# A new order at the entry of the second retrieval feed-forward's loop: copies taken earlier, four filler products, one table load ahead of a wait

## The chip, the cores and the metric

The kernel runs on one core of one Trainium2 chip. The metric is device microseconds of that core. Before the change three runs gave 1164.84, 1164.48 and 1162.4 us, median 1164.48 us. One further execution was profiled; the rows below are from it.

## The reference, cut to what matters

The program is four pairs of layers on x (16 sequences of 256 rows, 128 wide, f32): cross attention, then a feed-forward, each added to x after a layer norm. The change touches the entry of the third feed-forward, which the kernel calls `f2`:

```python
def _L2_ffn_ref(hidden_states, Wg, bg, Wu, bu, Wd, bd, Wq, keys, down_embed, up_embed):
    q = (hidden_states @ Wq).reshape(b, t, 2, H, RET // 2)
    sim = jnp.einsum('btphn,hkpn->pbthk', q, keys)
    sc, ix = jax.lax.top_k(sim, KPH)            # 8 best of 64, two sides, 4 heads
    ...
    all_sc = (sx[..., :, None] + sy[..., None, :]).reshape(b, t, H, KPH * KPH)
    scores, pk = jax.lax.top_k(all_sc, KPH)     # 8 best of the 64 pairs
    ...
    w = jnp.einsum('btd,bthkd->bthk', hidden_states, de)
    w = jax.nn.silu(w) * jax.nn.softmax(scores, axis=-1)
    experts_states = jnp.einsum('bthk,bthkd->btd', w, ue)
    mlp = jax.nn.silu(hidden_states @ Wg + bg) * (hidden_states @ Wu + bu) @ Wd + bd
    return mlp + experts_states
x = x + _L2_ffn_ref(_layernorm(x, axis=-1), ...)
```

Everything is f32 at this place. The work of later layers (attention `a3`, feed-forward `f3`) follows.

## The kernel before, in words

The 4096 rows are 32 tiles of 128 rows, and 8 groups of 4 tiles. The stages stand one behind the other in the program of each engine: `a2` (the attention ahead of `f2`), `f2`, `a3`, `f3`. Each engine runs its own program in the order in which it is written, and semaphores tie the engines together. There is no scheduler: the order in the code is the order on the engine.

In `f2` the work on a group g is spread over two turns of the loop. The *scores* of group g are made a turn ahead: TensorE multiplies the turned rows `hT` with `simw` (L1919, `sims` in `f2_pe`, four products, all through PSUM bank 0), ScalarE copies each from PSUM to SBUF (L2022, `sims` in `f2_act`), VectorE takes the eight best (L1838, L1850), GpSimd forms all sums of pairs (L2116, `pairs`), ScalarE takes exponentials (L2045, `exps`, four heads for each of four tiles), and VectorE weighs them (L2193, `weigh`). The *products* of group g (L1940, L1943, L1947 on TensorE, four columns c of three products) go to ScalarE for two Silu each (L2072, L2074) and to VectorE (L2228). GpSimd also folds the weighed exponentials (L2126, L2131) and adds the bias rows (L2137).

`groups2` runs the body in a loop for groups 0 to 5 (two to a pass) and then written out for groups 6 and 7. Ahead of it stands the entry, which is what the change touches:

- On TensorE: turning group 1's normalised rows (L336, `T(1, 1)`), then `sims(1, 1, t)` for t = 0 to 3. Each of these waits until ScalarE has emptied bank 0; the first waits for `hT`.
- On ScalarE: in `f2_first_act`, still in `a2`, three copies of `a3`'s values (L683). Then in `f2_act` `logs(0)` (L2027, L2031), `logz(0)` (L2035), and for each tile t the four exponentials of group 0 and behind them the copy `sims(1, t, 0)` (L2022). Behind the exponentials of tile 0 stand the end of a layer norm (L307, L310, L311), the fourth copy of `a3`'s values (L683) and `take_turned` (L341), which copies the turned rows from bank 0 to `hT`.
- On VectorE: `z`, `shift`, the rest of a layer norm (up to L293), `weigh(0, t)`; then the body, which begins with `top(1, 0)`.
- On GpSimd: 16 `pairs` of group 0, `bias(0)`, then folds and pairs in turn.

The functions Exp and Ln share one table of ScalarE, Silu is in another. Each body therefore loads a table twice: ahead of its first Silu (in the profile under L2072) and, through `preload_act_table_set`, behind its last (L2078).

Of the kernel before, what the change touches and what calls it, by code (L numbers as in the profile page):

```python
# [29 lines left out]
P = 128  # L30
# [3 lines left out]
GT = 4  # L34
# [44 lines left out]
def build(nc, dram):  # L79
    with ExitStack() as ctx:  # L80
        def sb(name, shape, dt=F32):
            return ctx.enter_context(nc.sbuf_tensor(name, shape, dt))
# [3 lines left out]
        def S(name):  # L86
            if name not in sems:
                sems[name] = ctx.enter_context(nc.semaphore(name))
            return sems[name]
# [24 lines left out]
        ident = W["ident"]  # L114
# [6 lines left out]
        simw = sb("simw", [P, 512])  # L121
# [25 lines left out]
        def bank(i):  # L147
            return psum[:, i, :]

        def tile_of(A, t):  # L150
            return A[:, ds(t, 1), :].rearrange("p a b -> p (a b)")
# [40 lines left out]
        def sem(s, name):  # L192
            return S("all_" + name)

        def at(s, name):
            return sum(count(x, name) for x in SUB[:SUB.index(s)])
# [142 lines left out]
        def take_turned(act, s, g, j):  # L339
            act.wait_ge(sem(s, "turned"), at(s, "turned") + g + 1 + 2)  # L340
            act.activation(hT[:, j, :], bank(0), ACT.Copy).then_inc(sem(s, "hT"), 1)  # L341
# [1567 lines left out]
        def f2_pe(pe, a3):  # L1909
            s = "f2"  # L1910
# [12 lines left out]
            for t in range(GT):  # L1923
                sims(1, 1, t)

            def dense_out(g, c):

                if c == 0:
                    pe.wait_ge(sem(s, "res"), at(s, "res") + g + 1)
                pe.wait_ge(S("f2_aT"), 4 * g + c + 1 + 1)  # L1930
                for t in range(GT):
                    pe.matmul(bank(7)[:, t * P:(t + 1) * P], aT[:, c, t * P:(t + 1) * P],
                              W["f2_wd"][:, c * P:(c + 1) * P], start=(t == 0 and c == 0), stop=False,
                              skip_group_check=True)
# [76 lines left out]
        def f2_act(act, a3):  # L2011
            s = "f2"
            act.sem_inc(S("f2_sl"), 1)
            act.sem_inc(S("f2_sg"), 1)

            def sims(G, t, before=None):
                act.wait_ge(S("f2_sim_ps"), 4 * G + t + 1)
                if before is not None:

                    act.wait_ge(S("f2_S"), 4 * before + t + 1)  # L2020
                    act.wait_ge(S("f2_t1"), 32 * before + 8 * t + 8)
                act.activation(sim[:, t * 512:(t + 1) * 512], bank(0), ACT.Copy).then_inc(S("f2_sim"), 1)  # L2022

            def logs(G):

                act.wait_ge(S("f2_m"), G + 1)
                act.activation(e8.rearrange("p t h k -> p (t h k)"), e8.rearrange("p t h k -> p (t h k)"), ACT.Exp)\  # L2027
                    .then_inc(S("f2_e8"), 1)
                if not (isinstance(G, int) and G == 0):
                    act.wait_ge(S("f2_mw"), 16 * G)  # L2030
                act.activation(best2, lead2, ACT.Copy).then_inc(S("f2_b2"), 1)  # L2031

            def logz(G):
                act.wait_ge(S("f2_z"), G + 1)
                act.activation(lnz2, z2, ACT.Ln).then_inc(S("f2_lnz"), 1)  # L2035

            def exps(G, t):

                if t == 0:
                    act.wait_ge(S("f2_shift"), G + 1)  # L2040
                act.wait_ge(S("f2_S"), 4 * G + t + 1)
                for h in range(NH2):
                    if not (isinstance(G, int) and G == 0 and 4 * t + h < 2):
                        act.wait_ge(S("f2_mw"), 16 * G + 4 * t + h - 1)
                    act.activation(bank(EX_BANK + h % 2), ssum[t][:, h * 512:(h + 1) * 512], ACT.Exp,  # L2045
                                   bias=shift2[:, t * NH2 + h:t * NH2 + h + 1]).then_inc(S("f2_ew"), 1)

            def norm(g, j):
                act.wait_ge(sem(s, "turned"), at(s, "turned") + g + 1)
                for t in range(GT):  # L2050
                    ins = act.activation(hrow[:, j, t * P:(t + 1) * P], tile_of(X, 4 * g + t), ACT.Identity,
                                         scale=rstd[:, ds(4 * g + t, 1)], bias=shifted[:, ds(4 * g + t, 1)])
                ins.then_inc(sem(s, "normed"), 1)

            logs(0)
            logz(0)
            for t in range(GT):
                exps(0, t)
                if t == 0:
                    ln_finish_act(act, s, 1)  # L2060
                    a3.values(3, 4)
                    take_turned(act, s, 1, 1)
                sims(1, t, 0)
            act.wait_ge(sem(s, "ln"), at(s, "ln") + 2 * LN_STEPS)

            def body(g, j, one_more, two_more):
                act.wait_ge(S("f2_pwT"), 4 * g + 1)
                for c in range(4):
                    act.wait_ge(S("f2_g_ps"), 4 * g + c + 1)
                    if c:  # L2070
                        act.wait_ge(S("f2_aT"), 4 * g + c)
                    act.activation(sl[c % 2], bank(3), ACT.Silu, bias=col("f2_bg%d" % c)).then_inc(S("f2_sl"), 1)  # L2072
                    act.wait_ge(S("f2_e_ps"), 4 * g + c + 1)
                    act.activation(sgT[:, c, :], bank(5), ACT.Silu).then_inc(S("f2_sg"), 1)  # L2074
                    if c == 1 and two_more:
                        norm(g + 2, j)
                if one_more:
                    act.preload_act_table_set("natural_log_exp_and_others")  # L2078
                if two_more:
                    take_turned(act, s, g + 2, j)  # L2080
                if one_more:
                    logs(g + 1)
                    logz(g + 1)
                if not one_more:
                    act.preload_act_table_set("natural_log_exp_and_others")
                    act.wait_ge(S("f2_S"), 4 * N_GROUPS)
                    act.wait_ge(S("f2_mw"), 16 * N_GROUPS)
                    a3.keys16(0)
                    take_turned(act, "a3", 0, 0)
                    a3.takeQ(0)  # L2090
                    a3.takeQ(1)
                    a3.keys16(1)
                    take_turned(act, "a3", 1, 1)
                    a3.takeN(0)
                for t in range(GT):
                    if one_more:
                        exps(g + 1, t)
                        if t == 0 and not two_more:
                            ln_finish_act(act, "a3", 0)
                    if two_more:  # L2100
                        sims(g + 2, t, g + 1)

            groups2(act, body)

        def f2_pool(pool):
# [869 lines left out]
```

## Time and profile before

| | |
|---|---|
| runs | 1162.4 to 1164.84 us, median 1164.48 |
| profiled execution | 1169.59 us, its span 1167.8 us |
| PE busy | 939.7 us, 80% |
| DVE busy | 836.0 us, 72% |
| ACT busy | 647.1 us, 55% |
| POOL busy | 464.6 us, 40% |

PE is TensorE, PEld its weight loads, DVE VectorE, ACT ScalarE, POOL GpSimd. Busy shares are averages over the whole span. `f2` lies between about 600 and 850 us of it, its entry between about 599 and 621 us. In a timeline, a row is: start in us, duration in us, engine, line, operation, output<-input with shapes, count; in square brackets the idle time before it and what ended that. Where instructions overlap in an engine's pipeline, a row's start can lie before the end of the row above.

### The profile page before, as it was taken

How to read it: one execution, taken by the hardware profiler on the slowest of the kernel's cores; microseconds unless marked ns; L12 is line 12 of the kernel's file. 1: busy time of each engine (PE TensorE's matmuls, PEld its weight loads, DVE VectorE, ACT ScalarE, POOL GpSimd, SP SyncE). 2: the span in 40 equal slices, each digit the busy share in tenths (PEclk: the TensorE clock that was granted, in tenths of full speed). 3: DMA queues.
4: the chain of work that ended last, by engine and by line, in shares of the span. 5: the costliest groups of instructions: out<-in, count | busy, mean ns of one | idle time of the engine just before them, and what ended most of it. 6: DMA issues, size and time to landing. Idle time of an engine off the chain costs nothing.

```text
span 1167.8 us, 21022 instructions
## 1 busy us (share of the span) xinstructions
PE 939.7 (80%) x7158; PEld 630.9 (54%) x7158; DVE 836.0 (72%) x2078; ACT 647.1 (55%) x1143; POOL 464.6 (40%) x446
## 2 busy tenths in 40 slices
PE   5958800578997998799859999998879988948987
PEld 3753300554555776355435767666645556527976
DVE  6785699857886666377778999999758885513443
ACT  4425578945653454566448778775456644104543
POOL 5500000001220001344369999998212242463655
PEclk9889955779999999799978999999979997978999
DMA  8000000055000000000000000000000000124431
GB/s 288 1 1 1 1 0 0 1 169 176 1 2 1 1 1 1 1 1 2 2 1 2 1 0 0 0 0 1 1 1 2 2 2 1 49 90 118 113 90 34
DMA packets 24233, 33.76 MB, mean 29 GB/s; under 512 B 3484, under 2 KB 20389, under 8 KB 23888
## 3 DMA queue, kind: packets, MB, share of 16 engines
q1 hardware_dynamic: 20720, 26.20, 7.3%
q0 software_dynamic: 3424, 6.38, 1.6%
q8 instruction: 55, 0.90, 0.3%
q14 instruction: 34, 0.28, 0.1%
HBM read 18.34 MB, written 15.98 MB: 29 GB/s over the span
## 4 chain that ended last, share of the span: by engine, by line
PE 35%; DVE 29%; issue 8%; ACT 5%; another core or an unknown queue 1%; POOL 1%; DVEq 1%; DMA 0%; POOLq 0%; ACTq 0%; SPq 0%
DVE big L850 7%; DVE hq L845 7%; PE psum L619 5%; PE psum L2534 5%; PE psum L1602 3%; ACT psum L2045 2%; DVE big L2193 2%; PE psum L2550 2%; PE psum L573 2%; PE psum L1619 2%; DVE big L854 2%; DVE psum L1850 1%; DVE tmp L1838 1%; DVE psum L1838 1%; PE psum L2436 1%
## 5 line engine op out<-in xcount | busy, mean ns | idle before, releaser
L845 DVE TENSOR_REDUCE hq<-psum 128x16 f32<-128x1024 f32 x96 | 114.5, 1220 | 82.1 <-PE psum L573 44.3
L2116 POOL TENSOR_TENSOR big<-big 128x512 f32<-128x512 f32 x128 | 128.7, 1050 | 7.0 <-ACT big L1878 7.0
L2193 DVE SCALAR_TENSOR_TENSOR big<-big,tmp,psum 128x512 f32<-128x512 f32 x128 | 90.4, 743 | 7.8 <-ACT psum L2045 4.7
L2045 ACT ACTIVATE psum<-big,tmp 128x512 f32<-128x512 f32 x128 | 84.9, 686 | 19.6 <-DVE big L2193 16.9
L735 ACT ACTIVATE big<-psum 128x1024 f32<-128x1024 f32 x64 | 62.0, 1021 | 54.6 <-PE psum L603 54.6
L850 DVE RECIPROCAL big<-psum 128x256 f32<-128x256 f32 x48 | 84.0, 1749 | 5.1 <-PE psum L619 4.9
L483 POOL TENSOR_TENSOR big<-big,w_const 128x256 f32<-128x256 f32 x32 | 24.0, 750 | 152.9 <-PE psum L619 145.8
L2721 DVE SCALAR_TENSOR_TENSOR big<-psum,big 128x128 f32<-128x128 f32 x118 | 36.0, 347 | 64.4 <-issue 45.3
L2126 POOL TENSOR_TENSOR big<-big 128x1024 f32<-128x1024 f32 x32 | 75.4, 2366 | 15.8 <-DVE big L2193 15.8
L1516 PE MATMUL psum<-f_downT,tmp 128*128 128x128 f32 x192 | 24.9, 294 | 68.0 <-DVE tmp L1399 68.0
L2414 POOL DMA_INDIRECT out<-big x59 | 57.9, 982 | 54.0 <-issue 34.2
L619 PE MATMUL psum<-big 128*32 128x256 f32 x768 | 52.3, 389 | 25.8 <-DVE big L854 25.7
L1285 DVE TENSOR_REDUCE amax<-big 128x1 f32<-128x1536 f32 x32 | 55.8, 1748 | 21.4 <-ACT big L1425 21.4
L599 PE MATMUL psum<-hq,big 32*128 32x256 f32 x768 | 65.6, 428 | 6.2 <-DVE hq L845 6.0
L341 ACT ACTIVATE hT<-psum 128x512 f32<-128x512 f32 x56 | 33.3, 595 | 58.0 <-PE psum L336 58.0
L2534 PE MATMUL psum<-tmp,big 128*128 x236 | 63.1, 391 | 0.9 <-ACT big L2581 0.8
L1516 PEld LDWEIGHTS psum<-f_downT,tmp 128*128 128x128 f32 x192 | 24.5, 210 | 68.8 <-DVE tmp L1399 68.3
L491 POOL TENSOR_TENSOR big<-big,w_a 128x256 f32<-128x256 f32 x16 | 11.7, 728 | 120.0 <-ACT big L707 120.0
L1258 POOL PARTITION_ALL_REDUCE qs<-qs x4 | 1.5, 371 | 144.7 <-DVEq L1238 131.1
L336 PE MATMUL psum<-w_const,hrow 128*128 128x128 f32 x224 | 37.4, 293 | 22.1 <-DVE hrow L1309 11.8
L483 POOL TENSOR_TENSOR big<-w_f,w_const 128x256 f32<-128x256 f32 x16 | 12.6, 791 | 105.5 <-PE psum L619 82.6
L1972 PEld LDWEIGHTS psum<-w_const,big 128*128 128x128 f32 x384 | 47.3, 196 | 8.6 <-issue 8.6
(334 smaller groups left out, 2629.2 us busy)
## 6 DMA issues: line engine op xcount, KB each, us to landing
rows<-pad SPq DMA_DIRECT2D x1, 7670.0 KB, 33.0
big<-rows SPq DMA_DIRECT2D x59, 130.0 KB
tmp<-in_pack_f SPq DMA_DIRECT2D x1, 2050.5 KB, 9.2
w_f<-in_pack_f SPq DMA_DIRECT2D x1, 1280.0 KB, 12.6
tmp<-in_pack_once SPq DMA_DIRECT2D x1, 960.0 KB, 7.1
out<-big POOLq DMA_INDIRECT x59
X<-in_x SPq DMA_DIRECT2D x1, 768.0 KB, 5.3
w_a<-in_pack_a SPq DMA_DIRECT2D x3, 256.0 KB, 8.1
```

The lines of the kernel that those rows point to most:

```text
L599: pe.matmul(bank(1 + r)[:, 256 * e:256 * e + 256], L.kbd[rows, b, e * P:(e + 1) * P], L.qT[b % L.ahead][rows, :], start=True, stop=False)
L619: ins = pe.matmul(bank(6)[32 * r:32 * r + 32, 256 * which:256 * which + 256], w, L.pt[b % 2][:, (2 * r + e) * 256:(2 * r + e + 1) * 256], ...
L735: act.activation(L.pt[b % 2][:, 1024 * half:1024 * half + 1024], psum[:, 1 + 2 * half:3 + 2 * half, :].rearrange("p c n -> p (c n)"), ACT.Exp,
L845: dve.tensor_reduce(nm, psum[:, 1 + 2 * t:3 + 2 * t, :].rearrange("p c (r l k) -> p (c r) l k", r=2, k=SK), AX.X, ALU.max, negate=True).th ...
L850: dve.reciprocal(L.rz, bank(6)[:, 256:512]).then_inc(hs("rz"), 1)
L1285: dve.tensor_reduce(amax[:, i, g:g + 1], A[:, g, :], AX.X, ALU.max, apply_absolute_value=True).then_inc(S("f0_am"), 1)
L2045: act.activation(bank(EX_BANK + h % 2), ssum[t][:, h * 512:(h + 1) * 512], ACT.Exp, bias=shift2[:, t * NH2 + h:t * NH2 + h + 1]).then_inc( ...
L2116: ins = pool.tensor_tensor(ssum[t][:, h * 512:(h + 1) * 512].rearrange("p (i j) -> p i j", i=ROWS2), st[:, 0, h, 0:ROWS2].unsqueeze(2).to_ ...
L2126: pool.tensor_tensor(ew[t][:, 0:left], ew[t][:, 0:left], ew[t][:, NFOLD * 512:], ALU.add)\
L2193: dve.scalar_tensor_tensor(out=ew[t][:, blk], in0=ssum[t][:, blk], scalar=best2[:, t, h, 7:8], in1=bank(EX_BANK + h % 2), op0=ALU.is_ge, o ...
L2414: pool.indirect_dma_start(dram["out"], bass.IndirectOffsetOnAxis(slot3[j % RS][:, ID3:ID3 + 1].bitcast(U32), 0), out3[j % RS], None, bound ...
L2534: ins = pe.matmul(bank(2 + j % 2)[:, 2 * P * k:2 * P * (k + 1)], hTb[j % 3], W["f3_w"][:, ds(weights_at(j, k), 2 * P)], start=True, stop=True)
```

## The change

It does three things. On ScalarE the fourth copy of values and `take_turned` move from behind the exponentials of tile 0 to the head of `f2_act`, the first copy `sims(1, 0, 0)` goes between `logs(0)` and `logz(0)`, and in the loop over tiles the copy of the next tile, not of the same, follows the exponentials. On TensorE four products of 256 columns into bank 6 follow the entry's `sims`; their result is not used. And each body of ScalarE begins with a load of the Silu table.

```diff
@@ f2_pe @@
             for t in range(GT):
                 sims(1, 1, t)
 
+            for _ in range(4):
+                pe.matmul(bank(6)[:, 0:2 * P], ident, simw[:, 0:2 * P], start=True, stop=True)
+
@@ f2_act @@
+            a3.values(3, 4)
+            take_turned(act, s, 1, 1)
             logs(0)
+            sims(1, 0, 0)
             logz(0)
             for t in range(GT):
                 exps(0, t)
                 if t == 0:
                     ln_finish_act(act, s, 1)
-                    a3.values(3, 4)
-                    take_turned(act, s, 1, 1)
-                sims(1, t, 0)
+                if t + 1 < GT:
+                    sims(1, t + 1, 0)
             act.wait_ge(sem(s, "ln"), at(s, "ln") + 2 * LN_STEPS)
 
             def body(g, j, one_more, two_more):
+                act.preload_act_table_set("silu_and_others")
                 act.wait_ge(S("f2_pwT"), 4 * g + 1)
```

On ScalarE, at the entry, this stood in a row before, up to the first copy of a score and not further (the three copies of values, L683, stand ahead of it, and after it exponentials and copies alternate; the last is a copy):

```order
L2027 ACTIVATE tmp<-tmp 128x128 [waits f2_m]
L2031 ACTIVATE tmp<-psum 128x128
L2035 ACTIVATE tmp<-tmp 128x16 [waits f2_z]
L2045 ACTIVATE psum<-big,tmp 128x512 [waits f2_S,f2_shift]
L2045 ACTIVATE psum<-big,tmp 128x512
L2045 ACTIVATE psum<-big,tmp 128x512 [waits f2_mw] x2
L307 ACTIVATE lnw<-lnw 128x8 [waits all_var]
L310 ACTIVATE psum<-lnw 128x8 [waits all_lnv]
L311 ACTIVATE lnw<-lnw 128x8
L683 ACTIVATE w_f<-psum 128x512 [waits att_v_ps]
L341 ACTIVATE hT<-psum 128x512 [waits all_turned]
L2022 ACTIVATE big<-psum 128x512 [waits f2_t1,f2_S,f2_sim_ps]
```

Line numbers of the changed kernel are up to 6 higher (L2025 is the copy, L2048 the exponential). There, at the same place, stands:

```order
L683 ACTIVATE w_f<-psum 128x512 [waits att_v_ps] x4
L341 ACTIVATE hT<-psum 128x512 [waits all_turned]
L2030 ACTIVATE tmp<-tmp 128x128 [waits f2_m]
L2034 ACTIVATE tmp<-psum 128x128
L2025 ACTIVATE big<-psum 128x512 [waits f2_t1,f2_S,f2_sim_ps]
L2038 ACTIVATE tmp<-tmp 128x16 [waits f2_z]
L2048 ACTIVATE psum<-big,tmp 128x512 [waits f2_S,f2_shift]
L2048 ACTIVATE psum<-big,tmp 128x512
L2048 ACTIVATE psum<-big,tmp 128x512 [waits f2_mw] x2
L307 ACTIVATE lnw<-lnw 128x8 [waits all_var]
L310 ACTIVATE psum<-lnw 128x8 [waits all_lnv]
L311 ACTIVATE lnw<-lnw 128x8
```

Three instructions (L683, L341 and the first copy) have moved ahead of the first exponential. Behind the exponentials of tile 0 only the layer norm's three stay, and behind those of tile 3 nothing stays.

Still on ScalarE, at the head of the loop's body, before:

```order
L163 UNCONDITIONAL_BRANCH [waits all_ln]
L163 ISA
L2072 ACT_TABLE_LOAD [waits f2_g_ps]
L2072 ACTIVATE big<-psum,w_const 128x512 [waits f2_pwT]
L2074 ACTIVATE big<-psum 128x512 [waits f2_e_ps]
```

And in the changed kernel (L2072 is now the line of the load itself, L2078 the Silu):

```order
L163 UNCONDITIONAL_BRANCH [waits all_ln]
L2072 ACT_TABLE_LOAD
L2073 ISA
L2078 ACTIVATE big<-psum,w_const 128x512 [waits f2_g_ps,f2_pwT]
L2080 ACTIVATE big<-psum 128x512 [waits f2_e_ps]
```

The load no longer waits for TensorE's first product (`f2_g_ps`); the number of loads is the same.

On TensorE, between the entry's score products and the loop:

```order
 L1919 MATMUL psum<-simw,hT 128x512 [waits f2_sim,all_hT] x4
+L1927 MATMUL psum<-simw,w_const 128x256 x4
 L163 UNCONDITIONAL_BRANCH [waits all_ln]
 L163 ISA
-L1940 MATMUL psum<-hT,w_f 128x512 [waits f2_sl]
+L1943 MATMUL psum<-hT,w_f 128x512 [waits f2_sl]
```

Nothing else of TensorE's order moves; the four fillers wait for nothing but their place in the queue. The orders of VectorE and GpSimd are as before.

## Rows read from the trace of the kernel before

**Rows 1.** The chain that ended last, in `f2`'s entry: start, us, what.
```profile
606.79 2.09 PE psum L1919 x2
...
619.80 0.85 ACT L2072
```

**Rows 2.** Timeline of ACT, the entry and the first body's load.
```profile
599.49 0.31 ACT L2027 ACTIVATE tmp<-tmp 128x128 f32<-128x128 f32 x1 [4.19 <-DVE tmp L1854]
...
601.67 0.22 ACT L2035 ACTIVATE tmp<-tmp 128x16 f32<-128x16 f32 x1 [1.71 <-DVE tmp L2177]
...
605.67 0.58 ACT L683 ACTIVATE w_f<-psum 128x512 f32<-128x512 f32 x1
606.15 0.59 ACT L341 ACTIVATE hT<-psum 128x512 f32<-128x512 f32 x1
608.90 0.60 ACT L2022 ACTIVATE big<-psum 128x512 f32<-128x512 f32 x1 [2.16 <-PE psum L1919]
609.39 1.29 ACT L2045 ACTIVATE psum<-big,tmp 128x512 f32<-128x512 f32 x2
...
618.83 0.58 ACT L2022 ACTIVATE big<-psum 128x512 f32<-128x512 f32 x1
619.80 1.28 ACT L2072 ACT_TABLE_LOAD   x1 [0.39 <-PE psum L1940]
```

**Rows 3.** Timeline of PE, the entry and group 0's first products.
```profile
597.69 0.60 PE L336 MATMUL psum<-w_const,hrow 128*128 128x128 f32 x4
606.79 2.08 PE L1919 MATMUL psum<-simw,hT 128*128 128x512 f32 x2 [8.49 <-ACT hT L341]
...
616.28 2.04 PE L1919 MATMUL psum<-simw,hT 128*128 128x512 f32 x2 [1.24 <-ACT big L2022]
618.11 1.60 PE L1940 MATMUL psum<-hT,w_f 128*128 128x512 f32 x2
...
621.83 1.13 PE L1940 MATMUL psum<-hT,w_f 128*128 128x512 f32 x2 [0.41 <-ACT big L2072]
622.80 1.02 PE L1943 MATMUL psum<-hT,w_f 128*128 128x512 f32 x2
```

**Rows 4.** Timeline of DVE, the entry and group 0's first product.
```profile
606.68 0.17 DVE L293 SCALAR_TENSOR_TENSOR lnw<-psum,lnw 128x8 f32<-128x8 f32 x1
610.19 0.75 DVE L2193 SCALAR_TENSOR_TENSOR big<-big,tmp,psum 128x512 f32<-128x512 f32 x1 [3.34 <-ACT psum L2045]
...
619.84 0.60 DVE L1838 MAX8 tmp<-big 128x8 f32<-128x64 f32 x4 [0.16 <-DVE big L2193]
...
621.91 0.75 DVE L2228 SCALAR_TENSOR_TENSOR big<-psum,w_const,big 128x512 f32<-128x512 f32 x1 [0.49 <-ACT big L2072]
```

**Rows 5.** Stretches: length, busy PE PEld DVE ACT POOL, granted clock, DMA share, GB/s.
```profile
598.00:600.00 2.00, 0.29 (x3) 0.05 (x1) 1.97 (x11) 0.47 (x2) 2.00 (x3) 0.70 0.00 0
618.00:620.00 2.00, 2.00 (x5) 0.89 (x4) 1.75 (x8) 1.61 (x4) 2.00 (x3) 0.68 0.02 4
858.00:860.00 2.00, 1.92 (x20) 1.52 (x24) 0.00 (x0) 0.70 (x2) 0.00 (x0) 0.50 0.04 8
```

**Rows 6.** Timeline of ACT, the loads of groups 1 and 7.
```profile
647.94 1.28 ACT L2072 ACT_TABLE_LOAD   x1
...
824.24 1.28 ACT L2072 ACT_TABLE_LOAD   x1 [1.75 <-PE psum L1940]
...
828.50 0.69 ACT L2072 ACTIVATE big<-psum,w_const 128x512 f32<-128x512 f32 x1 [1.79 <-PE psum L1940]
```

**Rows 7.** Timeline of POOL: folds of groups 0 and 1, bias of group 6.
```profile
613.21 2.36 POOL L2126 TENSOR_TENSOR big<-big 128x1024 f32<-128x1024 f32 x1 [4.70 <-DVE big L2193]
...
641.37 2.37 POOL L2126 TENSOR_TENSOR big<-big 128x1024 f32<-128x1024 f32 x1 [0.40 <-DVE big L2193]
...
807.66 1.27 POOL L2137 TENSOR_TENSOR X<-X,addrow 128x512 f32<-128x512 f32 x1
```

**Rows 8.** Timeline of DVE, behind the loop.
```profile
804.39 4.59 DVE L224 TENSOR_TENSOR lnw<-stats 128x20 f32<-128x20 f32 x1
```

## The prediction

> **What bounds the kernel now.** I read the chain of waits first. In the entry of `f2` it runs from ScalarE's copy of the turned rows into TensorE's first score product at 606.79 and ends, after copies, exponentials and products, in the table load at 619.80 [rows 1]. ScalarE's timeline shows why: ScalarE is idle 4.19 us ahead of `logs(0)` and 1.71 us ahead of `logz(0)`; then, behind the exponentials of tile 0, it copies values (605.67) and the turned rows (606.15), waits 2.16 us for the product that those rows feed, and copies that (608.90), before the exponentials of tile 1 start at 609.39 [rows 2]. So work that could have been done in an idle stretch stands between two exponentials. TensorE had the turned rows ready at 597.69 + 0.60 = 598.29 and then sat 8.49 us [rows 3]. VectorE waited 3.34 us for the exponential [rows 4], and GpSimd 4.70 us for VectorE [rows 7]. All four engines wait for this one detour. It happens once, not in each group.
>
> **The moved copies: what goes.** All times in this part are of the profiled execution.
>
> Values and turned rows. TensorE has long finished the values' product, and the turned rows are ready at 598.29. Both copies (0.58 and 0.59 us [rows 2]) fit into the 4.19 us in which ScalarE waits for VectorE: the turned rows' copy then runs from 598.35 to about 598.95, and `logs(0)` still starts at 599.49. Price: nothing, cover 0.5 us.
>
> The first score. TensorE starts it 0.05 us behind the copy, as it does now (606.15 + 0.59 = 606.74, start 606.79 [rows 2, 3]), so at 599.0. The granted clock falls within 598 to 600 (mean 0.70 [rows 5]), so I take the slower level, as today: from the product's start to the copy's start 608.90 - 606.79 = 2.11 us. The copy starts at 601.1, the next instruction 0.49 us behind (608.90 to 609.39), at 601.6. `logz(0)` waits for VectorE until 601.67 anyway [rows 2]. Hidden, but with 0.1 us of cover only; the bounds are 0 and +0.3 us (a product that starts a few tenths late). I take 0.
>
> Tile 0 to tile 1. The exponentials of tile 0 and the layer norm's three stay where they are, up to 605.67. Now the copy of tile 1's score comes, whose product has been done since 603.8 (it follows the first copy), and 0.49 us later, at 606.16, the exponentials of tile 1 start, instead of at 609.39: 3.23 us earlier. VectorE is free then: its layer norm ends at 606.68 + 0.17 = 606.85 [rows 4], and the exponential's first result comes at about 606.9, 0.8 us behind its start as today (609.39 to 610.19). Tiles 2 and 3 keep their pace, since their products of 2.1 us stand beside 3.3 us of exponentials.
>
> The end. The last copy (618.83, 0.58 us) is gone from behind tile 3, and so is the 0.39 us that the load waited for TensorE's first product [rows 2], if that product is there. ScalarE can load at 618.83 - 3.23 = 615.60 instead of 619.80: 4.20 us. The first Silu follows at 616.9 instead of 619.80 + 1.28 = 621.1.
>
> **Who is late next.** TensorE starts its fourth score product behind the copy ahead of tile 2's exponentials, at about 609.7 (now 616.28), done at 611.7. Then come the fillers. At the slower level the fourth score product took 618.11 - 616.28 = 1.83 us to the next one's start, 512 columns [rows 3]; four fillers of 256 columns are worth two such, 3.7 us, so at worst they end at 615.3. The loop's first product, another 1.8 us at that level, is then ready at 617.1, against a Silu at 616.9: 0.2 us at worst. But the clock should rise in the meantime. It rose from 1.2 to 2.4 GHz within 618 to 620 (mean 0.68 [rows 5]), while TensorE worked without a gap from 616.28 on. Here it works without a gap from 609.7 on, so I expect full clock while the fillers run, these done by about 614 and the three products of column 0 by about 616.6. The fillers stand in time in which TensorE would wait: they cost nothing, and gain little, as the clock would have risen on column 0's products too.
>
> VectorE has gained only 3.24 us: its `top(1, 0)` starts at 616.6 and takes until 618.2 (619.84 to 621.91 - 0.49 = 621.42 now [rows 4]), and group 0's first sum of products starts there instead of at 621.91: 3.7 us. TensorE's second column waits for the Silu and starts at 617.65 instead of 621.83 [rows 3]: 4.2 us. Nothing of TensorE waits for VectorE's first sum until four products later, and from 622 to 634 TensorE has no gap at all in the chain, so TensorE's 4.2 us count; VectorE makes up its 0.5 us out of 0.25 to 0.65 us waits that it has later in the group.
>
> GpSimd gains 3.3 us at its second fold (613.21) and runs without a gap from there to 641.37, where it waits 0.40 us for VectorE [rows 7]. It waits so at this fold in each group. So it is 0.9 us behind the others in group 0 and has made that up by group 2. No engine waits for it inside the loop: the list of waits from 620 to 820 us has no row with GpSimd as the releaser.
>
> **The table load ahead of the wait.** Load and Silu need each other only through ScalarE's own queue. In group 1 the load stands without idle time ahead of it (647.94 [rows 6]); it is so in groups 1 to 6, six loads. Putting it ahead of a wait that is already fulfilled gives nothing there. In group 0 the wait was the 0.39 us counted above. In group 7 the load waited 1.75 us for TensorE (824.24) and would now be done first, so the Silu comes 1.28 us earlier. But the Silu's own followers don't wait for it: TensorE has `a3`'s four key products behind column 0, and ScalarE's next Silu waits 1.79 us for TensorE [rows 6]. Value: 0, with bounds 0 and -1.3 us.
>
> The load takes 1.28 us in all rows, and the next instruction starts 0.01 us behind it. The Trainium skill, "ScalarE: Activation LUTs", section "What ACT_TABLE_LOAD costs", gives 1283 ns for the load and 1380 ns of drain, 2.66 us for each switch. The trace agrees on the load and shows no drain ahead of the 647.94 one. By that page hiding it in group 7 could be worth 2.66 us of ScalarE's time there.
>
> **Sum.** -3.23 (tile 1) - 0.58 (last copy) - 0.39 (wait) = -4.2 us for ScalarE and TensorE; +0.1 for the two places with hardly any cover. -4.1 us. Behind the loop VectorE is held 4.59 us at 804.39 [rows 8] until GpSimd's last instruction of the loop ends at 807.66 + 1.27 = 808.93 [rows 7]; as GpSimd has caught up by then, this shifts with the rest. What comes later depends on data alone and shifts too. On the profiled execution's own time 1169.59 becomes 1165.5; that execution lies 5.1 us over the median of the runs, so 1164.48 becomes 1160.4 us.
>
> **Rivals.**
>
> A. GpSimd decides. If its few tenths of slack are not there in the changed loop, its end at 808.93 moves only by the 3.3 us that it gains at its second fold, and VectorE behind it likewise: 1161.2 us. For it speaks that GpSimd works 641.37 - 0.40 - 613.21 = 27.8 us of a group of 647.94 - 619.80 = 28.1 us [rows 2, 6, 7]. Against it: the wait of 0.40 us, which comes again in each group. The Trainium skill, "SBUF — State Buffer", section "SBUF: two separate sides", gives the rule behind the held instruction: a VectorE operation with two inputs in SBUF and a GpSimd operation take one port pair, and the later one blocks. By that rule GpSimd's end sets VectorE's start at 808.93, which the rows bear out to 0.05 us.
>
> B. The gain is given back later. TensorE's clock changes level a dozen times between 800 and 1060 us, and each change can come a microsecond or so earlier or later against the shifted work. Half of the 4.1 us lost that way: 1162.5 us, no difference that can be told.
>
> C. The clock stays low. Column 0's last product then ends at 615.3 + 3 x 1.8 = 620.7, the second column starts 1.1 us earlier than now, and from there each 0.86 us product takes 1.72. If that holds through columns 1 to 3, nine products, it costs 7.7 us: -1.1 + 7.7 = +6.6, 1171 us, slower. It decides once the low level lasts beyond about 627.5 us (6.8 us, 3.4 us lost). For it: in 858 to 860 us TensorE was busy 1.92 of 2 us and still at 0.50 [rows 5], and a gap of 1 us waits at 616.6. Against it: that stretch had gaps around it, and in groups 1 to 6 gaps of 0.7 us left the clock at full.
>
> D. The load is worth more than I think: if ahead of the wait it hid in all eight groups, 7 x 1.28 = 9 us more, 1151 us. Against it: no idle time ahead of six of the loads.
>
> **How the numbers follow.** What a measurement of this kernel can tell is about 0.2%, 2.3 us, so faster means under 1162.2. Chances: my forecast (1159 to 1162) 0.70; A 0.09; B 0.13; C 0.04; D 0.03; nothing reaches the end at all 0.01. Forecast, A and D are faster, 0.82; B and the last mostly the same, 0.13 with a little left over; slower is C with a part of B's outcomes, 0.05. The range: the forecast with the bounds of the uncovered places (+0.3) and of group 7 (-1.3), a microsecond of scatter in the medians on either side, and up to B: 1157.8 to 1163.2.
>
> **What would show it.** In the changed profile: the turned rows' copy at about 598.4, the first score's copy at 601.1 ahead of `logz(0)`, tile 1's exponentials at 606.2, the load at 615.6 with no idle time ahead, the first Silu at 616.9; GpSimd's second fold at about 610; group 1's load at 643.7 (now 647.94); VectorE's held instruction at 800.2. I am wrong if `logz(0)` starts more than 0.3 us late, if the granted clock is at 0.50 beyond 617, or if the group from 643.7 on is longer than the 28.1 us of the group before it now.

## The result and the profile after

The changed kernel took 1158.60 us in the median of 8 runs (1154.26 to 1160.51), the kernel before 1163.45 us in 8 (1162.40 to 1164.87). The ratio is 0.9954, its 95% interval 0.9941 to 0.9966. So it is faster by 5.4 us (4.0 to 6.9), or 4.85 us from median to median; 4.1 us were forecast. The median of 1158.60 us lies within the range that was stated (1157.8 to 1163.2), but 0.4 us under the band of 1159 to 1162 us that was given the chance of 0.70; the kernel before came out 1.0 us under the median from which the forecast counted. Two later comparisons of the same kernel gave 0.9968 (0.9957 to 0.9980) and 0.9957 (0.9942 to 0.9972), 3.7 and 5.0 us.

The profiled execution took 1160.51 us, its span 1158.7 us. It is 9.1 us under the profiled execution of before, but that difference is not to be read as the change's: the kernel before, profiled again, took 1162.21 us (span 1160.4 us), 1.7 us more than the changed kernel's profile, which reached `f2` later. The first profile of before held stalls worth some 7 us behind 995 us that the second does not have (experiment 5). In the entry the two profiles agree to 0.01 us.

Executions differ ahead of `f2`: the changed kernel reaches its head 2.5 us later than before in this profile, the same kernel in experiment 12 0.2 us later, and over all fourteen profiles the start of `logs(0)` lies between 599.2 and 602.0 us. I therefore count from the start of `logs(0)` (599.49 before, 601.99 after). These are the rows of ScalarE after that answer to [rows 2] (start, us, operation, in brackets idle time before):

```profile
600.83 0.60 ACT L341 ACTIVATE hT<-psum 128x512 f32<-128x512 f32 x1 [2.16 <-PE psum L336]
601.99 0.31 ACT L2030 ACTIVATE tmp<-tmp 128x128 f32<-128x128 f32 x1 [0.56 <-DVE tmp L1854]
...
603.59 0.60 ACT L2025 ACTIVATE big<-psum 128x512 f32<-128x512 f32 x1 [1.12 <-PE psum L1919]
604.18 0.22 ACT L2038 ACTIVATE tmp<-tmp 128x16 f32<-128x16 f32 x1
...
608.18 0.58 ACT L2025 ACTIVATE big<-psum 128x512 f32<-128x512 f32 x1
608.66 1.29 ACT L2048 ACTIVATE psum<-big,tmp 128x512 f32<-128x512 f32 x2
...
618.18 1.28 ACT L2072 ACT_TABLE_LOAD   x1
619.48 0.69 ACT L2078 ACTIVATE big<-psum,w_const 128x512 f32<-128x512 f32 x1
...
646.52 1.28 ACT L2072 ACT_TABLE_LOAD   x1
```

The 2.16 us of waiting between two exponentials are gone. (The 2.16 us in the first row are another wait, for TensorE to turn the rows, in a stretch in which ScalarE would wait for VectorE anyway; that the two numbers are alike is chance.) And `logz(0)` (L2038) follows `logs(0)` by 2.19 us as against 2.18 us before. On TensorE, to set beside [rows 3]:

```profile
601.48 2.08 PE L1919 MATMUL psum<-simw,hT 128*128 128x512 f32 x2 [0.69 <-ACT hT L341]
...
612.26 2.04 PE L1919 MATMUL psum<-simw,hT 128*128 128x512 f32 x2 [1.31 <-ACT big L2025]
614.10 3.62 PE L1927 MATMUL psum<-simw,w_const 128*128 128x256 f32 x8
617.51 1.44 PE L1943 MATMUL psum<-hT,w_f 128*128 128x512 f32 x2
...
620.51 1.02 PE L1943 MATMUL psum<-hT,w_f 128*128 128x512 f32 x2
```

The fillers (L1927) and the loop's first products run without a gap, and the second column's product at 620.51 follows them with no wait: here TensorE, not the Silu at 619.48 + 0.69 = 620.17, decides. The chain of waits after says the same (start, us, what):

```profile
612.26 2.04 PE psum L1919 x2
614.31 3.41 PE psum L1927 x8
617.72 1.24 PE psum L1943 x2
```

The fillers stand on the chain, the list of waits that ended last. The clock, to set beside [rows 5] (length, busy time of PE, PEld, DVE, ACT, POOL, granted clock, DMA share, GB/s):

```profile
616.00:618.00 2.00, 2.00 (x6) 1.50 (x5) 1.90 (x5) 1.78 (x3) 2.00 (x3) 0.50 0.01 4
618.00:620.00 2.00, 2.00 (x5) 0.76 (x4) 1.84 (x11) 1.97 (x3) 2.00 (x2) 0.91 0.00 0
```

It rose only at about 618.4 (the mean of 0.91 over 618 to 620 puts it at 618.36), behind the fillers. GpSimd, to set beside [rows 7]; the line of the folds is now L2132:

```profile
637.86 4.69 POOL L2132 TENSOR_TENSOR big<-big 128x1024 f32<-128x1024 f32 x2
...
668.15 2.37 POOL L2132 TENSOR_TENSOR big<-big 128x1024 f32<-128x1024 f32 x1 [0.19 <-DVE big L2199]
...
696.95 2.38 POOL L2132 TENSOR_TENSOR big<-big 128x1024 f32<-128x1024 f32 x1 [1.01 <-DVE big L2199]
```

At this fold GpSimd has no wait in group 1, 0.19 us in group 2 and 1.01 us in group 3; before the change these waits were 0.40, 0.42 and 1.01 us. So it was behind, and from group 3 on it had caught up in full. And the held instruction behind the loop, to set beside [rows 8]:

```profile
803.00 4.56 DVE L224 TENSOR_TENSOR lnw<-stats 128x20 f32<-128x20 f32 x1
```

It came 803.00 - 601.99 = 201.01 us behind `logs(0)`, before 804.39 - 599.49 = 204.90 us: 3.9 us earlier, all that the entry gave.

### The profile page after: what moved, and what is told of

Same layout as the page of the kernel before. It is cut to its first block, busy times and chain, and to the rows that moved or that the text cites. A ratio compares the mean times of both kernels' runs of the same rounds, so it can differ in the third digit from the quotient of the medians.

```text
span 1158.7 us, 21041 instructions
## 1 busy us (share of the span) xinstructions
PE 945.0 (82%) x7166; PEld 635.6 (55%) x7166; DVE 835.1 (72%) x2078; ACT 648.0 (56%) x1143; POOL 465.2 (40%) x446
## 4 chain that ended last, share of the span: by engine, by line
PE 34%; DVE 28%; issue 8%; ACT 4%; POOL 3%; DVEq 0%; DMA 0%; POOLq 0%; ACTq 0%
DVE big L850 7%; DVE hq L845 7%; PE psum L619 5%; PE psum L2540 5%; PE psum L1602 3%; POOL rows L2410 3%; DVE big L2199 2%; PE psum L2556 2%; ACT psum L2048 2%; PE psum L573 2%; PE psum L1619 2%; DVE big L854 2%; DVE tmp L1838 1%; DVE psum L1838 1%; DVE psum L1850 1%
## 5 line engine op out<-in xcount | busy, mean ns | idle before, releaser
L2048 ACT ACTIVATE psum<-big,tmp 128x512 f32<-128x512 f32 x128 | 85.0, 686 | 19.5 <-DVE big L2199 16.9
L2132 POOL TENSOR_TENSOR big<-big 128x1024 f32<-128x1024 f32 x32 | 75.2, 2361 | 12.0 <-DVE big L2199 12.0
L341 ACT ACTIVATE hT<-psum 128x512 f32<-128x512 f32 x56 | 33.3, 595 | 60.6 <-PE psum L336 60.6
```

What stands on the lines that cost most here:

```text
L2132: pool.tensor_tensor(ew[t][:, 0:left], ew[t][:, 0:left], ew[t][:, NFOLD * 512:], ALU.add)\
```

## The experiments

Twelve runs follow: eight other kernels (one of them twice), the whole change twice more, and the kernel before once more. One number reads each of them sharply: the *entry*, from the start of `logs(0)` to the table load of group 1. It holds the entry and group 0. It was 48.45 us in both profiles of before (647.94 - 599.49) and 44.53, 44.51 and 44.51 us in the three of the change, so it repeats to 0.02 us, while the times of one kernel scatter by 3 us or more. The next column, *to the end*, is the profile's span less the start of `logs(0)`, against 1160.4 - 599.54 = 560.9 us in the second profile of before; it shows what of the entry's difference is left when the kernel ends, to some 0.4 us.

| | kernel | entry, us | against before, us | to the end, against before, us | time over before (95% interval), us |
|---|---|---|---|---|---|
| 5 | before | 48.45, 48.45 | | 560.9 us | |
| | whole change | 44.53 | -3.92 | -4.2 | -5.4 (-6.9 to -4.0) |
| 1 | order alone | 44.33 | -4.12 | -4.4 | -4.0 (-5.6 to -2.4) |
| 2 | fillers alone | 51.46 | +3.01 | +3.0 | +0.7 (-0.3 to +1.7) |
| 3 | load alone | 48.10 | -0.35 | -0.8 | -0.6 (-1.6 to +0.5) |
| 4 | whole change | 44.51 | -3.94 | -4.0 | -3.7 (-5.0 to -2.3) |
| 6 | old order, 16 fillers | 55.34 | +6.89 | +6.9 | +7.4 (+5.9 to +8.8) |
| 7 | new order, 16 fillers | 50.37 | +1.92 | +0.1 | +0.8 (-0.1 to +1.9) |
| 8 | new order, copies between | 44.21 | -4.24 | -4.1 | -3.7 (-5.1 to -2.4) |
| 9 | early take alone | 45.24 | -3.21 | -3.3 | -3.0 (-4.2 to -1.7) |
| 10 | fillers alone | 50.91 | +2.46 | +0.8 | -0.3 (-1.4 to +0.7) |
| 11 | order and load | 44.33 | -4.12 | -4.2 | -4.2 (-5.7 to -2.7) |
| 12 | whole change | 44.51 | -3.94 | -4.1 | -5.0 (-6.7 to -3.3) |

**1. The order alone.** The four fillers and the early load are left out of the changed kernel:

```diff
-            for _ in range(4):
-                pe.matmul(bank(6)[:, 0:2 * P], ident, simw[:, 0:2 * P], start=True, stop=True)
...
-                act.preload_act_table_set("silu_and_others")
```

> Only the order on ScalarE is changed; no fillers, no load ahead of the wait. The entry is measured from the start of logs(0) to the table load of group 1: 48.45 us before, 44.53 us in the changed kernel. Theory 1 (the order is the whole gain, the fillers lie in waiting time): entry 44.4 to 44.6 us, time 3.5 to 4.5 us under before. Theory 2 (the fillers raise TensorE's clock in time and carry part of it): the first Silu or the second column's product comes later without them, entry 45.0 us or more. Theory 3 (the part of the gain beyond 4.1 us comes from later stalls that depend on how many instructions the streams hold): the entry is short, but the time differs from the whole change's by 1 us or more.

Entry 44.33 us, time -4.0 us. The order is the whole gain of the entry, and the entry is 0.2 us shorter without the other two parts. The time differs from the whole change's by 1.4 us in the first comparison, but by 0.3 us beside experiment 4, on the same chip, so nothing speaks for theory 3. TensorE's rows of this kernel (`logs(0)` is at 600.87):

```profile
612.98 1.91 PE L1940 MATMUL psum<-hT,w_f 128*128 128x512 f32 x2
614.69 1.91 PE L1943 MATMUL psum<-hT,w_f 128*128 128x512 f32 x2
616.40 1.45 PE L1947 MATMUL psum<-hT,w_f 128*128 128x512 f32 x2
619.09 1.12 PE L1940 MATMUL psum<-hT,w_f 128*128 128x512 f32 x2 [1.25 <-ACT big L2074]
```

The clock rises at about 617.2, 16.4 us behind `logs(0)`; with the fillers it rises 16.4 us behind it too (618.36 - 601.99). So they did not bring it up earlier. Without them the first column's products run at 1.2 GHz, and are still done 1.25 us before the Silu lets the second column start. The second column starts 18.22 us behind `logs(0)`, with fillers 18.52 us.

**2. The fillers alone**, in the old order:

```diff
             for t in range(GT):
                 sims(1, 1, t)
 
+            for _ in range(4):
+                pe.matmul(bank(6)[:, 0:2 * P], ident, simw[:, 0:2 * P], start=True, stop=True)
+
```

> Only the four filler products, in the old order. There the loop's first product stands right behind the fourth score product and the table load waits for it (0.39 us). Theory 1: the fillers now stand on the chain and cost up to their length: entry longer by 1.5 to 3 us than 48.45, time slower by as much. Theory 2 (the clock rises earlier and pays them back): entry within 0.5 us of 48.45.

Entry 51.46 us, 3.0 us longer. The load's row says where they stand:

```profile
622.96 1.28 ACT L2075 ACT_TABLE_LOAD   x1 [3.38 <-PE psum L1943]
```

It waits 3.38 us for the first product, before 0.39 us. Theory 1 holds in the entry. But the time is only 0.7 us over before, and 3.0 us lies outside the interval. See 6 and 10. In this profile the clock also stood elsewhere, and that before any filler had run. These are stretches of experiment 2, and below them one of before (columns as in [rows 5]):

```profile
600.00:601.00 1.00, 0.00 (x0) 0.00 (x0) 0.96 (x5) 0.12 (x1) 1.00 (x2) 1.00 0.00 0
621.00:622.00 1.00, 1.00 (x4) 0.82 (x3) 0.55 (x3) 0.00 (x0) 1.00 (x1) 0.50 0.00 0
```

```profile
600.00:601.00 1.00, 0.00 (x0) 0.00 (x0) 0.93 (x5) 0.00 (x0) 1.00 (x2) 0.50 0.00 0
```

Before, the granted clock falls 0.7 us ahead of `logs(0)` and rises 19.8 us behind it; here it falls 1.9 us behind it, while TensorE waits for the turned rows as before, and rises 22.4 us behind it. The low stretch is as long as before, 20.5 us, but lies later. So all four fillers and the start of column 0 ran at 1.2 GHz. The late fall cannot come from the fillers, the first of which starts at 618.28.

**3. The load alone**, in the old order:

```diff
             def body(g, j, one_more, two_more):
+                act.preload_act_table_set("silu_and_others")
                 act.wait_ge(S("f2_pwT"), 4 * g + 1)
```

> Only the table load ahead of the wait. Theory 1: it hides 1.28 us plus the wait of 0.39 us at the first body at most where TensorE's first product is late, in group 7 1.28 us on ScalarE that nobody waits for; entry 48.0 to 48.45 us or, as the Silu then waits for the product's end at 619.7 instead of for the load's end at 621.1, 47.1 us; time 0 to 1.4 us under before. Rival D of the prediction: 1.28 us in each group, 9 us under before.

```profile
619.38 0.58 ACT L2022 ACTIVATE big<-psum 128x512 f32<-128x512 f32 x1
619.98 1.28 ACT L2067 ACT_TABLE_LOAD   x1
621.27 0.69 ACT L2073 ACTIVATE big<-psum,w_const 128x512 f32<-128x512 f32 x1
...
648.12 1.28 ACT L2067 ACT_TABLE_LOAD   x1
```

The load follows the copy without a wait, 0.35 us earlier than before, and that is all that it gives: 48.10 us. The 9 us of rival D are not there.

**4. The whole change again**, unchanged.

> The whole change again, for a second profile and beside the parts on the same chip. Entry 44.5 us. Theory 1: 4 to 5 us under before. The stalls behind 1010 us (ScalarE and VectorE waiting for neither a semaphore nor data) differ between executions of the same kernel by more than 1 us if they are not due to the change.

Entry 44.51 us, time -3.7 us. From 995 us on its stretches are as long as those of the first profile after, to 0.3 us: the changed kernel does not differ from itself there.

**5. The kernel before again**, unchanged, for a second profile.

> The kernel before, profiled a second time. Entry 48.4 to 48.5 us (table load of group 1 less start of logs(0)). The stall of 11.5 us on VectorE at 1018 us stood only in the first profile of it, not in those of the changed kernels. Theory 1 (it is an accident of that execution): it is missing here. Theory 3 (the change took it away): it is here again.

The first profile of before had this in 1015 to 1034 us (engine and line, who was waited for, total, times, longest; *remote* says that the profile shows no instruction that ended the wait):

```profile
ACT big L2559 <- remote: 12.2, 1, 12.2
DVE big L2655 <- remote: 11.5, 1, 11.5
```

The second has no such row, nor has any of the other twelve profiles. Between 996 and 1059 us the same instructions of VectorE take 63.1 us in the first profile of before, 59.2 in the second and 59.1 in the first profile after, as most of the 11.5 us is made up behind it; two smaller stalls between 1059 and 1125 us add 3.3 us. They belong to one execution, and the change did not take them away. What held the engines is not shown.

**6. Sixteen fillers in the old order.** As experiment 2, with `range(16)`.

> Sixteen fillers in the old order of ScalarE, where they stand on the chain. Four cost 3.0 us of the entry, but only 0.7 us (-0.3 to 1.7) of the time. Twelve more cost 24 half-size products at 0.21 us, 5.2 us of the entry: entry 56.6 us. If what the entry loses is lost at the end, the time is 8.2 us over before; if about 2.3 us are given back whatever the loss, 5.9 us over; if three quarters are given back, 2 us over.

```profile
618.50 7.62 PE L1927 MATMUL psum<-simw,w_const 128*128 128x256 f32 x32
```

Entry 55.34 us, 6.9 us longer; I had said 8.2, by adding to experiment 2, in which the clock rose 22.4 us behind `logs(0)`; here it rose 19.7 us behind it, as before, so that fewer products ran at 1.2 GHz. The time is 7.4 us over before (5.9 to 8.8). This loss arrives in full, in the profile too (6.9 us to the end).

**7. Sixteen fillers in the new order**, without the early load.

> Sixteen fillers in the new order, without the load ahead of the wait. They start some 5 us ahead of the place where they stand in the old order, so part of them lies in TensorE's waiting time. Theory 1 (fillers cost what reaches beyond the first Silu): 10 of 32 half-size products at 0.43 us, 22 at 0.21 us, 9 us, of which 3.4 us are covered; entry 49.5 to 50.5 us; time 1 to 2 us over before. Rival (the engine only wants to be kept busy, and more fillers bring the clock up earlier): entry under 47 us.

```profile
623.80 1.28 ACT L2077 ACT_TABLE_LOAD   x1 [6.05 <-PE psum L1943]
```

Entry 50.37 us. The load waits 6.05 us for the first product: the fillers cost what reaches beyond the moment at which ScalarE is ready, 50.37 - 44.33 = 6.0 us. The clock rose 16.4 us behind `logs(0)` as with four or none. Rival fallen. But of the entry's 1.92 us next to nothing reaches the end. It is there up to the exponentials ahead of group 7 and is lost at that group's table load, which has no wait here and waits 1.76 us for TensorE in the second profile of before. `f2`'s last residual starts 853.08 - 601.58 = 251.50 us behind `logs(0)`, in the second profile of before 850.80 - 599.54 = 251.26 us:

```profile
853.08 0.69 DVE L349 TENSOR_TENSOR X<-X,psum 128x512 f32<-128x512 f32 x1 [0.30 <-PE psum L1983]
```

Ahead of group 7's load the clock is low once for 6.8 us, from 210.9 us behind `logs(0)`; before it is low twice for 3.4 us, from 210.9 and from 221.2 us. The second of those lies on products that TensorE runs without a gap, and here these run at 2.4 GHz. That this gives the 1.7 us back is argued from the profile; no run isolates it.

**8. The copies between the exponentials.** From experiment 1, the copy of tile t's score now stands in the middle of tile t's exponentials:

```diff
-                exps(0, t)
+                exps(0, t, (lambda: sims(1, t, 0)) if t else None)
...
-                if t + 1 < GT:
-                    sims(1, t + 1, 0)
```

> The new order alone (no fillers, no early load), and the copies for tiles 1 to 3 stand between the second and the third exponential of their tile, where ScalarE waits 0.2 to 0.5 us for VectorE, not ahead of the first. Theory 1 (the entry is then bound by VectorE's weighing, 3.0 us a tile in place of 3.28): entry 43.8 to 44.1 us, 0.3 to 0.5 us under the new order alone, whose entry is 44.33 us. Rival (the score product is late for its copy and holds the third exponential): entry as it is or longer.

```profile
611.08 0.57 ACT L2022 ACTIVATE big<-psum 128x512 f32<-128x512 f32 x1
611.56 1.29 ACT L2045 ACTIVATE psum<-big,tmp 128x512 f32<-128x512 f32 x2
...
614.36 0.58 ACT L2022 ACTIVATE big<-psum 128x512 f32<-128x512 f32 x1
```

Entry 44.21 us, 0.12 us under the new order alone. A tile still takes 614.36 - 611.08 = 3.28 us. My theory fell: the wait of 0.2 us was filled, but a new one of 0.2 to 0.3 us appeared ahead of the other pair. Its time does not differ from the new order's.

**9. The early take alone.** The copies of values and turned rows move to the head; the score copies stay behind their own tile's exponentials:

```diff
+            a3.values(3, 4)
+            take_turned(act, s, 1, 1)
             logs(0)
             logz(0)
             for t in range(GT):
                 exps(0, t)
                 if t == 0:
                     ln_finish_act(act, s, 1)
-                    a3.values(3, 4)
-                    take_turned(act, s, 1, 1)
                 sims(1, t, 0)
```

> Only the copies of values and of the turned rows move to the head; the four copies of scores stay each behind the exponentials of their own tile. The sum of the prediction gives this part 0.48 + 0.49 + 2.16 = 3.13 us and leaves the last copy (0.58 us), the load's wait (0.39 us) and the copy's 0.1 us for the other part. Entry 48.45 - 3.13 = 45.3 us. Rival (the score copies' new place is what counts, the early take alone only moves the wait): entry 47 us or more. Time 2 to 4 us under before.

```profile
605.40 0.58 ACT L2022 ACTIVATE big<-psum 128x512 f32<-128x512 f32 x1
605.88 1.29 ACT L2045 ACTIVATE psum<-big,tmp 128x512 f32<-128x512 f32 x2
...
616.31 1.28 ACT L2072 ACT_TABLE_LOAD   x1 [0.41 <-PE psum L1940]
```

Entry 45.24 us, -3.21 as against -3.13 forecast for this part. The load still waits 0.41 us for TensorE's first product, which stands behind the fourth score product, and that starts only when the third copy has emptied bank 0. The other part of the order is thus worth 45.24 - 44.33 = 0.9 us (0.58 + 0.39 forecast).

**10. The four fillers in the old order, again**, on another chip.

> The four fillers in the old order, once more, on another chip. The entry was 3.0 us longer, the time only 0.7 us (-0.3 to 1.7) above, while sixteen fillers gave 6.9 us and 7.5 us. If every loss of the entry arrives at the end, the time is about 3 us over before (1.5 to 4). If the four fillers are paid back elsewhere, it is again within 1 us.

Entry 2.5 us longer in the profile, time -0.3 us (-1.4 to +0.7). The expectation that every loss arrives at the end failed a second time. The traces explain a part. As in experiment 2, the clock fell later than in the profiles of before (0.8 us behind `logs(0)`) and rose later (21.3 us), so more of the work ran at 1.2 GHz. Had it risen where it did in experiment 6, eight half-size products would have taken 2.3 us in place of 3.4, and the entry would have been some 1.7 us longer; this is an estimate, from that run's rise at 19.7 us, its first filler at 18.6 us, 0.43 and 0.21 us a product and 1.1 us from column 0's first product to the load. And in this profile only 0.8 of the 2.5 us is left at `f2`'s last residual and at the end, with the same single low stretch of 6.8 us as in experiment 7, while in experiment 2 all 3.0 us arrive. The two profiled executions, 1165.25 and 1164.84 us, were the longest and the second longest of their eleven. The other twenty were not seen: what the four fillers cost in them, between nothing and 1.7 us, stays open.

**11. Order and load, without fillers.**

> The new order with the early load, without the fillers. The new order alone has an entry of 44.33 us, and its load has no idle time ahead of it, so that the early load has nothing to hide: entry 44.3 us, 0.2 us under the whole change, whose fillers hold the second column's product 0.3 us. If the early load matters beside the new order: entry under 44.1 us. Time as the whole change.

Entry 44.33 us, as with the order alone. Beside the new order the early load has nothing to hide. In this profile the clock fell 5.3 us behind `logs(0)` and rose 15.5 us behind it, in experiment 1 it is 0.7 us ahead and 16.4 us behind; the entry is the same, since column 0's products have 1.25 us to spare there.

**12. The whole change, a third time.**

> The whole change a third time, beside its parts. Entry 44.5 us. The first comparison gave 5.4 us under before, the second 3.7 us. If the gain is the entry's alone, 3.5 to 4.5 us.

Entry 44.51 us, time -5.0 us. Over the three comparisons the whole change ran 21 times. Three of these took 1154.3 to 1154.5 us with a mean granted clock of 0.919; the other eighteen, at 0.911 to 0.913, have a median of 1159.4 us, some 4 us under the medians of before beside them (1163.2 to 1163.6). Of before, 68 executions are on record, none under 1161 us, and the clock is known for 60 of them, 0.908 to 0.915. Two of the three fast ones lie in the first comparison, and without them its median is 4.2 us under before. In this one they explain nothing: without its fast one the median is 1158.4 us, still 5.1 us under. None of the three was profiled. The nearest that was is experiment 9's profile, at 0.917 the shortest of its eight: its clock is low for 112.6 us ahead of `logs(0)`, against 126.3 us in the first profile after, and behind `logs(0)` for as long as there (82.3 against 81.6 us). So there the higher clock belongs to the work ahead of `f2`, which the change does not touch; and executions at 0.916 came in the old order too (experiment 3, two of eleven).

## Why the prediction was right, step by step

*Values and turned rows at no price.* Right: `logs(0)` still waits 0.56 us for VectorE behind them, 0.5 us of cover were forecast.

*The first score hidden behind `logz(0)`.* Right, to 0.01 us (2.19 against 2.18 us).

*3.23 us between tile 0 and tile 1.* Right. Tile 1's exponentials start 608.66 - 601.99 = 6.67 us behind `logs(0)`, before 609.39 - 599.49 = 9.90: 3.23 us. Experiment 9 splits it off.

*4.2 us at the load.* Right, to 0.1 us. The load is at 16.19 us after, at 20.31 before: 4.12 us. The first Silu is at 17.49 against 21.60 us, 4.11 us.

*The clock rises while the fillers run; they cost nothing.* This step failed. The rise came 6.1 us after TensorE had begun to work without a gap at 612.26, in the kernel before 3.0 us after 616.28 [rows 3, 5], and in experiment 2 5.6 us; I had read one distance from one case. At 1.2 GHz the fillers take 3.4 us of the chain. The second column, which I had at 617.65 - 599.49 = 18.16 us behind `logs(0)`, starts at 18.52 us, right behind the first column's last product; that product was to be done at 616.6, 17.1 us behind `logs(0)`. In experiment 1, without fillers, the Silu lets the second column start at 18.22 us. The worst case that I had worked out for the first product (0.2 us) did not matter; the third product's end did, and I had taken that for safe. The price is 0.2 us of the entry. The sign that I had named, a clock at 0.50 beyond 617 (17.5 us behind `logs(0)`), did not come: it rose at 16.4 us. That sign was set too late to catch this error. The miss stayed small because without the fillers column 0 has 1.25 us to spare (experiment 1), of which they use up all and 0.3 us more.

*VectorE makes up its half microsecond, GpSimd its 0.9 us by group 2.* Right: VectorE's first sum is 3.7 us early, as forecast, the start of group 1 3.9 us; GpSimd's waits are 0, 0.19 and 1.01 us in groups 1 to 3. No engine waited for it, and the held instruction moved with the rest. The Trainium skill, "SBUF — State Buffer", section "SBUF: two separate sides", says that of the two engines the one whose instruction starts first has the shared port pair for that whole instruction, and that the other blocks. After the change L224 ends at 803.00 + 4.56 = 807.56, GpSimd's last instruction of the loop at 807.50, so the trace agrees that VectorE was blocked; but it was held for more than one instruction, through the one that ran at 803.00 and four more that followed back to back. Rival A, which would have GpSimd's lag pass through, fell.

*The early load gives nothing in groups 1 to 6 and in group 7.* Right, and rival D is refuted by experiment 3. Group 7's load and first Silu after:

```profile
821.09 1.28 ACT L2072 ACT_TABLE_LOAD   x1
822.38 0.69 ACT L2078 ACTIVATE big<-psum,w_const 128x512 f32<-128x512 f32 x1
...
827.10 0.69 ACT L2078 ACTIVATE big<-psum,w_const 128x512 f32<-128x512 f32 x1 [2.84 <-PE psum L1943]
```

The Silu starts without a wait, and ScalarE then waits 2.84 us for TensorE's second column, before 1.79 us [rows 6]: the 1.1 us only changed places. The instruction behind the load starts 1.29 us behind its start, so nothing of the drain of 1380 ns that "ScalarE: Activation LUTs", section "What ACT_TABLE_LOAD costs", of the Trainium skill adds shows here either.

*The gain reaches the end; rival B.* Right as a sum, though parts of the time moved between stages. These are two instructions of VectorE in the second profile of before and in the profile after, the first at `f2`'s last residual, the second in the last attention block:

```profile
850.80 0.69 DVE L349 TENSOR_TENSOR X<-X,psum 128x512 f32<-128x512 f32 x1 [0.31 <-PE psum L1980]
...
960.35 1.76 DVE L850 RECIPROCAL big<-psum 128x256 f32<-128x256 f32 x1 [0.64 <-PE psum L619]
```

```profile
849.33 0.69 DVE L349 TENSOR_TENSOR X<-X,psum 128x512 f32<-128x512 f32 x1 [0.31 <-PE psum L1983]
...
960.25 1.76 DVE L850 RECIPROCAL big<-psum 128x256 f32<-128x256 f32 x1 [0.64 <-PE psum L619]
```

The stretch between them is 109.55 us before and 110.92 after: `a3` gives 1.4 us back, and in this profile the clock has one more low stretch, 3.4 us from 272.4 us behind `logs(0)`, than before. Wherever a profile has this one more, `a3` takes 110.9 to 111.1 us (experiments 1, 4, 8, 10 and 12); where it has not, 109.4 to 109.6 us (2, 6, 7, 9 and 11); in experiment 3 it is low there for 6.8 us, and `a3` takes 112.4. The next stretches, up to 1016 us, take 1.6 us less, and from the residual to the instruction at 1016 us it is 165.0 us before, 164.8 after and 164.7 to 165.1 in the profiles of all twelve experiments. So the clock shifts time between stages there but takes none of the gain. From `logs(0)` to the end of the span the three profiles of the change take 4.0 to 4.2 us less than the second of before, which is what was forecast. Rival B was not empty, though: in experiments 7 and 10 1.7 us of a loss did not arrive, and nothing in the prediction says why a gain should be safe from that.

*The size.* 4.1 us forecast, 4.85 us by the medians, 5.4 by the ratio. The entry accounts for 3.9 us, the profiles from `logs(0)` to the end for 4.0 to 4.2. What the first comparison shows beyond that is mostly in its two executions at 0.919, which the prediction had no case for; the 5.0 us of experiment 12 is not explained by them and lies within its interval (3.3 to 6.7). The lower end of the range also comes to 1160.4 - 1.3 - 1.0 = 1158.1 us by the terms that the prediction names, not to 1157.8; the result is inside either way.

## What to carry to other kernels

A copy that another engine's first product waits for belongs in the last idle stretch ahead of it: one such move was worth 3.2 us, with 0.5 us of idle time to spare. Filler products that are meant to keep TensorE's clock up must be priced at the slow clock, up to the end of the last product that the next stage needs, and compared with what the real work would have done in their place; here real work was there, and they only delayed it. For differences of a few tenths of a microsecond measure an interval inside the profile, between two instructions of one engine, and look at what is left of the difference at the end as well, since 1.7 us of it went missing in two profiles here; and take a second profile of the kernel before, since a single one can hold an accident as large as the change.

## What the runs showed that I had not expected

In the new order the granted clock fell 0.7 us ahead of `logs(0)` and rose 16.3 to 16.4 us behind it in six profiles, with no filler (experiments 1 and 8), four (the whole change, three times) or sixteen (7), though TensorE's work differed. In the old order it fell at the same place and rose 19.7 to 19.8 us behind it with no filler (before, twice, and experiment 3) or sixteen (6). The exceptions are experiments 2, 10 and 11, where it had fallen later, before any filler ran, and experiment 9 (0.5 us ahead, 16.6 us behind). In no pair that fell at the same place did the fillers bring the rise forward by more than 0.1 us. Which place an execution gets is not explained by the kernel's code: before and experiment 2 have the same program up to there.

Four fillers that cost 2.5 to 3.0 us of the entry in two profiles cost nothing that could be measured in 22 executions, and sixteen cost all of theirs. Both profiles with four fillers were taken from executions in which the clock had fallen late, which it did in none of the seven other profiles on that chip and in one of the three on the other; whether it did so in the twenty executions that were not profiled is not known.
